# Signed adjacency copies picked by GpSimd in place of mask products on TensorE, in a four-layer graph network

## The chip, the cores and the metric

The kernel runs on one core of one Trainium2 chip. The metric is the device time of one execution in microseconds. A core has five engines that run side by side and meet at semaphores: TensorE (PE, matmuls into PSUM), VectorE (DVE), ScalarE (ACT), GpSimd (POOL) and SyncE (SP), which here issues all transfers.

## What is computed

32 graphs of 512 nodes with 256 features pass through four residual layers, each `x = x + layer(relu(layernorm(x)), adj)`, all in float32.

```python
# layer 0: (adj @ h + eps*h) @ W1 + b1 -> RMS norm -> silu -> @ W2 + b2       (W1: 256 -> 1024)
# layer 1: att = sigmoid(s1_i + s2_j) * adj * mask; rows normalised; att @ (h @ W.T + b)
# layer 2: 8 heads of 32 features:
scores = einsum('bhid,bhjd->bhij', q, k) / sqrt(HD) + edge_bias       # edge_bias = adj * W_e[head]
scores = where(adj_mask[:, None], scores, -inf)                       # adj_mask: adj != 0
attn   = softmax(scores); out = (attn @ v) @ W_o.T
# layer 3: d_i^-1/2 adj_ij d_j^-1/2 @ (h @ weight) + bias,  d = row sums of adj
```

The change concerns the edge bias and the mask of layer 2: a score gets W_e[head] times the adjacency value, and where the adjacency is zero it has to vanish from the softmax.

## The kernel before

A batch element (one graph) goes through a front half (layers 0 and 1) and a back half (layers 2 and 3). A phase works on three batch elements at once: the back half of t, the front half of tf = t + 1, and the load, norm and aggregation of nx = t + 2. There are 33 phases, those in the middle in a hardware loop. There is no scheduler: in each engine's block a function `phases(t, tf, nx)` calls the steps in an order written out by hand, and each engine runs its own list strictly in that order, with semaphore waits in between. So a step that waits holds up everything behind it on its engine.

The middle of a phase is a grid of 36 steps g = -4 to 31. At step g PE computes score tile g + 4 (head (g+4)//4, 128 rows, 512 columns) into one of two score banks, DVE's `bias` adds the adjacency, multiplies by the head's weight and takes the row extreme, ACT's `exps` makes the exponential, and PE turns tile g of the probabilities (`turn_probs`, four 128x128 transposes; a head's turns need all its four exps). ACT copies three of four turned tiles to `pT`, DVE the fourth. After head 3 and after head 7 the tiles are multiplied with the values (`attend`). Between these, the feed-forward part of layer 0 for tf runs in four tiles n, whose step u = g + 4 - 8n says what is due: hidden products at 0 and 1, squares on ACT, the norm factor on POOL (`hidden_norm`), `hidden` on DVE at 3, tanh and silu at 4 and 5, transposes of the hidden tile at 5 and 6, high and low halves at 6 and 7, down products in four quarters from 11, `update0` at 15. The last tile has its four quarters all at u = 8.

A score tile is two products, one for q k and one for the mask, which adds a huge value where the adjacency is zero. Its sign is the sign of the head's weight, because DVE's `bias` later multiplies the sum by that weight (`neg_w`) and takes a minimum:

```python
pe.matmul(SB_[i % 2][:, :], qk_stack[:, h % 4, 0, tile(n)], qk_stack[:, h % 4, 1, :], start=True, stop=False)
pe.matmul(SB_[i % 2][:, :], neg_mask[:, h, :], unlinked[:, n, :],
          start=False, stop=True).then_inc(sc_ps, 1)
```

`neg_mask` is a diagonal matrix per head, `unlinked` a bfloat16 map of the zero entries, made once per batch by `graph(t)` on DVE together with the row sums `deg`. The q and k of a head are stacked in four row groups by four SyncE transfers per head (`stack`), into one of four slots.

After the grid comes a stretch without scores: turn of the inverse sums, `attend(1)`, `project_o`, layer 1 of tf (`attend1`, `linear`), layer 3 of t (`aggregate3`, `project3`), the aggregation of nx in two halves (`aggregate(nx, 0)`, `aggregate(nx, 1)`), and the turn of hf for the next back half. Then the next phase begins with `project_qk`, `hidden(tf, 0, ...)` and `project_v`.

## Time and profile before

| | |
|---|---|
| median of 3 runs | 3797.84 us (3796.89 to 3798.93) |
| the profiled execution | 3793.83 us, its span 3792.0 us |
| PE busy | 3595.9 us, 95% |
| DVE busy | 2623.7 us, 69% |
| ACT busy | 2279.2 us, 60% |
| POOL busy | 772.2 us, 20% |
| mean granted clock of TensorE | 0.996 |

The span goes from the first to the last instruction of the core; 1.8 us of the execution's time lie around it. Busy shares overlap, since the engines work side by side. A matmul's duration in the trace runs from its issue to its modelled end, so for pipelined matmuls the distance from start to start says what one costs.

### The profile page before, as it was taken

The page shows a single profiled execution, that of the slowest core. Times are in us where ns is not written, and L with a number is a line of the kernel's source. Part 1 is how long each engine was busy: PE and PEld are TensorE (multiplying, and loading weights), DVE is VectorE, ACT ScalarE, POOL GpSimd, SP SyncE. Part 2 cuts the span into 40 slices and gives each one's busy share as a digit, 9 for nine tenths or more (in the row PEclk, how much of TensorE's full clock was granted, in tenths as well). Part 3 has the DMA queues.
Part 4 walks back from the last instruction along what each step waited for, and adds up shares of the span by engine and source line. Part 5 has one row for each costly group of instructions (what it writes and reads, how often), then busy time and mean ns, then how long its engine had stood idle before and what let it go on. Part 6 is the DMA issues. An engine that isn't in the chain of part 4 may idle for free.

```text
span 3792.0 us, 67268 instructions
## 1 busy us (share of the span) xinstructions
PE 3595.9 (95%) x19375; PEld 2445.7 (64%) x19596; DVE 2623.7 (69%) x6436; ACT 2279.2 (60%) x5029; POOL 772.2 (20%) x1611
## 2 busy tenths in 40 slices
PE   4899999999999999999999999999999999999997
PEld 3566666666666666666666666666666666666664
DVE  4676776666767766767767766667677667677664
ACT  2565666555666656666656665556666566666564
POOL 1122211222212222212222112222122222122210
PEclk9999999999999999999999999999999999999999
DMA  2232132322232322223321323222323222233212
GB/s 85 62 85 72 56 89 56 89 74 69 67 78 67 89 67 67 78 57 87 85 71 56 89 56 89 75 70 67 78 67 89 67 67 78 57 87 85 65 45 67
DMA packets 166936, 275.09 MB, mean 73 GB/s; under 512 B 23906, under 2 KB 59874, under 8 KB 166756
## 3 DMA queue, kind: packets, MB, share of 16 engines
q1 hardware_dynamic: 166756, 273.45, 26.7%
q14 instruction: 160, 1.31, 0.1%
q8 instruction: 20, 0.33, 0.0%
HBM read 122.37 MB, written 16.78 MB: 37 GB/s over the span
## 4 chain that ended last, share of the span: by engine, by line
PE 61%; issue 13%; DVE 12%; POOL 8%; ACT 5%; POOLq 0%; DMA 0%; DVEq 0%; SPq 0%; another core or an unknown queue 0%; ACTq 0%
PE turn L1213 9%; PE front L1026 7%; PE score L1203 6%; PE front L1027 6%; PE front L1028 6%; PE score L1204 4%; PE value L1228 3%; POOL small L374 3%; PE front L1056 3%; PE front L1079 3%; PE score L1177 3%; PE value L1189 3%; DVE pT L813 2%; ACT hf L500 2%; PE front L1068 2%
## 5 line engine op out<-in xcount | busy, mean ns | idle before, releaser
L588 ACT ACTIVATE prob<-prob,small 128x512 f32<-128x512 f32 x1024 | 736.1, 719 | 375.4 <-DVE small L888 373.8
L888 DVE CUSTOM_DVE_ANT_0 prob<-score,adj_sb,drv 128x512 f32<-128x512 f32 x1024 | 759.4, 747 | 224.8 <-PE score L1204 126.9
L1213 PE MATMUL turn<-ident,prob 128*128 128x128 f32 x4096 | 617.1, 276 | 14.6 <-ACT pT L597 8.7
L1213 PEld LDWEIGHTS turn<-ident,prob 128*128 128x128 f32 x4096 | 484.9, 141 | 134.8 <-issue 62.0
L597 ACT ACTIVATE pT<-turn 128x512 f32<-128x512 f32 x768 | 446.5, 584 | 144.6 <-PE turn L1213 144.6
L1203 PE MATMUL score<-qk_stack 128*128 128x512 f32 x1024 | 496.0, 488 | 31.5 <-DVE small L888 29.9
L1026 PE MATMUL front<-w_hi,s_hi 128*128 128x256 f32 x1024 | 353.0, 345 | 28.6 <-DVE x_in L792 28.6
L1204 PE MATMUL score<-unlinked,neg_mask 128*128 128x512 bf16 x803 | 313.6, 391 | 0.0
L680 DVE TENSOR_TENSOR s_lo<-front,s_hi 128x512 fp32r<-128x512 f32 x320 | 217.7, 680 | 102.7 <-ACT s_hi L486 102.6
L1027 PE MATMUL front<-w_lo,s_hi 128*128 128x256 f32 x1024 | 288.0, 281 | 0.0
L1028 PE MATMUL front<-w_hi,s_lo 128*128 128x256 f32 x1024 | 287.6, 281 | 0.0
L1026 PEld LDWEIGHTS front<-w_hi,s_hi 128*128 128x128 f32 x1024 | 196.0, 191 | 114.2 <-issue 52.6
L1228 PE MATMUL value<-pT,vals 128*32 128x512 f32 x2048 | 252.9, 600 | 5.1 <-issue 5.1
L421 POOL TENSOR_TENSOR inv_x<-small,drv 128x128 f32<-128x128 f32 x256 | 94.7, 401 | 784.0 <-DVE small L904 784.0
L1056 PE MATMUL front<-adjT_f,hid 128*128 128x512 f32 x512 | 232.0, 596 | 20.2 <-ACT hid L500 18.0
L486 ACT ACTIVATE s_hi<-front 128x512 fp32r<-128x512 f32 x320 | 187.5, 586 | 98.4 <-PE front L1111 94.5
L398 POOL TENSOR_TENSOR small<-small 128x1 f32<-128x1 f32 x128 | 24.7, 193 | 1083.3 <-ACT aside L529 1083.3
L773 DVE SCALAR_TENSOR_TENSOR hid<-front,small,rmsw_b 128x512 f32<-128x512 f32 x256 | 180.1, 745 | 88.8 <-POOL small L402 88.8
L1254 PE MATMUL score<-prob,hb 128*128 128x512 f32 x512 | 234.3, 601 | 4.5 <-ACT hb L500 4.5
L1203 PEld LDWEIGHTS score<-qk_stack 128*128 128x128 f32 x1024 | 195.0, 190 | 60.2 <-DVE small L888 54.5
L1111 PE MATMUL front<-pT,hf 128*128 128x512 f32 x512 | 227.5, 597 | 1.6 <-DVE pT L813 1.6
L897 DVE COPY pT<-turn 128x512 f32<-128x512 f32 x256 | 175.9, 687 | 75.8 <-PE turn L1213 73.9
(160 smaller groups left out, 7447.2 us busy)
## 6 DMA issues: line engine op xcount, KB each, us to landing
qk_stack<-qk SPq DMA_DIRECT2D x1024, 128.0 KB, 2.4
adjT_f<-in_adjT SPq DMA_DIRECT2D x32, 1024.0 KB, 5.0
adj_sb<-in_adj SPq DMA_DIRECT2D x32, 1024.0 KB, 7.9
prob<-in_adjT SPq DMA_DIRECT2D x32, 1024.0 KB, 5.4
x_new<-in_x SPq DMA_DIRECT2D x32, 512.0 KB, 3.7
out<-x_out SPq DMA_DIRECT2D x32, 512.0 KB, 3.1
pT<-in_W SPq DMA_DIRECT2D x2, 1024.0 KB
rmsw_b<-in_rmsw SPq DMA_DIRECT2D x1, 512.0 KB
```

What stands on the lines that cost most here:

```text
L588: act.activation(prob[:, i % 8, :], prob[:, i % 8, :], ACT.Exp, bias=nmax[:, h, n:n + 1], scale=-1.0, accum_out=prsum[:, h, n:n + 1]).then ...
L597: act.activation(pT[:, h % HG, j, :], TB[k % 2][:, :], ACT.Copy).then_inc(pT_act, 1)
L888: dve.tensor_tensor_reduce(out=prob[:, i % 8, :], in0=SB_[i % 2][:, :], in1=adj_sb[:, n, :], scale=neg_w[:, h:h + 1], scalar=3e38, op0=ALU ...
L1026: pe.matmul(ps, a[0], b[0], start=start, stop=False)
L1027: pe.matmul(ps, a[0], b[1], start=False, stop=False)
L1028: return pe.matmul(ps, a[1], b[0], start=False, stop=stop)
L1056: last = pe.matmul(FB[d][:, :], h0[:, m, tile(d)], adjT_f[:, m, :], start=(m == 0), stop=(m == NT - 1))
L1203: pe.matmul(SB_[i % 2][:, :], qk_stack[:, h % 4, 0, tile(n)], qk_stack[:, h % 4, 1, :], start=True, stop=False)
L1204: pe.matmul(SB_[i % 2][:, :], neg_mask[:, h, :], unlinked[:, n, :], start=False, stop=True).then_inc(sc_ps, 1)
L1213: last = pe.transpose(TB[k % 2][:, tile(n)], prob[:, (4 * h + n) % 8, tile(j)], ident[:, :])
L1228: last = pe.matmul(VB[HD * h:HD * h + HD, :], vals[:, j, P * g + HD * h:P * g + HD * h + HD], pT[:, h, j, :], start=(j == 0), stop=(j == N ...
L1254: last = pe.matmul(SB_[d][:, :], hb[:, m, tile(d)], adjT_b[:, m, :], start=(m == 0), stop=(m == NT - 1))
```

## The change

`unlinked`, `neg_mask` and the mask product go. Instead DVE makes two maps per batch, both with the adjacency where there is an edge, and where there is none +1e37 in one and -1e37 in the other. They stand side by side in `edges`; the loaded adjacency itself is turned into one of them. For each of the 32 score tiles GpSimd copies the tile of the map that fits the sign of the head's weight (`below`, read once into registers) into one of three buffers `edge`, and `bias` adds that. The row sums and the maps are made at the end of the phase before, when the element is still tf.

Further: `tile_steps` begins two steps earlier (u = g + 6 - 8n) with the transposes of the hidden tile at 6 and 7 and its halves at 7 and 8, and the last tile's quarters are spread over two steps; `aggregate(nx, 1)` moves from the end of a phase to behind `project_qk(tf, 0, ...)` of the next; `project_v(t, 1)` moves to step -2; `project_qk` writes into the turn banks; q and k of the second group of heads come a step later; there are three stack slots instead of four; `x_new` lies in a part of `pT`, so that the load of x waits for the last `attend`, behind the stack transfers and the two adjacency loads in SyncE's order; and `restore_diagonal` moves with the aggregation. Cut to the core:

```diff
         x2 = sb("x2", [P, NT, D])
-        adj_sb = sb("adj_sb", [P, NT, N])
-        unlinked = sb("unlinked", [P, NT, N], BF16)
+        edges = sb("edges", [P, 2, NT, N])
+        adj_sb, edges_neg = edges[:, 0, :, :], edges[:, 1, :, :]
+        edge = sb("edge", [P, 3, N])
         hb = sb("hb", [P, NT, D])
         bT = sb("bT", [P, DT, N])
         qk = sb("qk", [P, 4, N], F32R)
         x_out = sb("x_out", [P, NT, D], over="qk")
-        qk_stack = sb("qk_stack", [P, 4, 2, N], F32R)
+        qk_stack = sb("qk_stack", [P, 3, 2, N], F32R)
         vals = sb("vals", [P, NT, D])
         a3_hi = sb("a3_hi", [P, DT, N], F32R, over="vals")
...
-            return [(n, g + 4 - 8 * n) for n in range(NT) if 0 <= g + 4 - 8 * n < 16]
+            return [(n, g + 6 - 8 * n) for n in range(NT) if 0 <= g + 6 - 8 * n < 17]
         def quarters(n, u):
             if n == NT - 1:
-                return range(4) if u == 8 else ()
+                return (2 * u - 18, 2 * u - 17) if u in (9, 10) else ()
             return (u - 11,) if 11 <= u < 15 else ()
         GRID = range(-4, 4 * H)
-        Q1_STEP, K1_STEP = 0, 3
+        Q1_STEP, K1_STEP = 1, 4
+        def stack_slot(h):
+            return h % 3, 64 * (3, 3, 2)[h % 3], 64 * (h // 3 + 1)
         def linear_bank(n):
...
-            def back2(t):
...
@@ -314,6 +310,15 @@
                     if tf is not None:
                         load_adj(tf)
                 if nx is not None:
+                    sp.wait_ge(b2_added, at(tf, 1, 1))
+                    unregistered(sp)
+                    sp.wait_ge(f_norm["ready"], at(tf, 8, 4))
+                    unregistered(sp)
+                    if t is not None:
+                        sp.wait_ge(av_ps, at(t, 8, 8))
+                        unregistered(sp)
+                    load_x(nx)
                     sp.wait_ge(att_ready, at(tf, 4, 4))
                     unregistered(sp)
...
                 pool.wait_ge(deg_ready, at(t, 1, 1))
+                if later(t):
+                    pool.wait_ge(out_ready, at(t, 4, 0))
                 pool.tensor_tensor(dege, deg, wide(k_deg, NT), ALU.add).then_inc(deg_eps, 1)
                 pool.wait_ge(deg_eps, at(t, 1, 1))
                 pool.tensor_tensor(dinv, dege, wide(k_mhalf, NT), ALU.pow).then_inc(dinv_ready, 1)
+            def pick_edges(t, i):
+                h, n = divmod(i, NT)
+                if h == 0:
+                    pool.wait_ge(edges_ready, at(t, 4, n + 1))
+                if i >= 3:
+                    pool.wait_ge(biased, at(t, 32, i - 2))
+                elif later(t):
+                    pool.wait_ge(out_ready, at(t, 4, 0))
+                unregistered(pool)
+                pool.tensor_copy(edge[:, i % 3, :], edges[:, bass.ds(sign_of[h], 1), n, :].rearrange("p o n -> p (o n)")).then_inc(edge_picked, 1)
             def widen_inverse(t, g):
...
             def phases(t, tf, nx):
-                if t is not None:
+                b, f = t is not None, tf is not None
+                if b:
+                    for i in range(3):
+                        pick_edges(t, i)
                     degrees(t)
-                if tf is not None:
+                if f:
                     hidden_norm(tf, 0)
-                    hidden_norm(tf, 1)
-                if t is not None:
-                    widen_inverse(t, 0)
-                if tf is not None:
-                    hidden_norm(tf, 2)
-                    hidden_norm(tf, 3)
+                for i in range(3, 4 * H):
+                    if b:
+                        pick_edges(t, i)
+                    if f and i % 8 == 2 and i >= 8:
+                        hidden_norm(tf, i // 8)
+                    if b and i == 21:
+                        widen_inverse(t, 0)
                 if t is not None:
                     widen_inverse(t, 1)
...
                     act.wait_ge(av_ps, at(t, 8, j + 1))
+                if h == HG - 1 and j == 0:
+                    act.wait_ge(b2_added, B if isinstance(t, int) and t > B - 3 else at(t, 1, 2))
...
                 if f:
+                    aggregated(tf, 1)
+                if b:
+                    values(t, 0)
+                if f:
                     square(tf, 0, 0)
-                if b:
-                    values(t, 0)
-                if f:
                     square(tf, 0, 1)
-                if b:
-                    values(t, 1)
                 for g in GRID:
                     if f:
                         for n, u in tile_steps(g):
@@ -620,10 +647,12 @@
                                 square(tf, n, u - 1)
                             elif u in (4, 5):
                                 tanh(tf, n, u - 4)
-                            elif u in (6, 7):
-                                hidden_hi(tf, n, u - 6)
+                            elif u in (7, 8):
+                                hidden_hi(tf, n, u - 7)
                     if b and g + 4 < 4 * H:
                         exps(t, g + 4)
+                    if b and g == -2:
+                        values(t, 1)
                     if b and g >= 0 and g % 4 != DVE_TURN:
                         turned_probs(t, g // 4, g % 4)
...
-            def graph(t):
-                dve.wait_ge(adj_loaded, at(t, 16, 16))
-                if later(t):
-                    dve.wait_ge(sc_ps, at(t, 32, 0))
-                    dve.wait_ge(dinv_ready, at(t, 1, 0))
-                dve.tensor_scalar(unlinked[:, :, :], adj_sb[:, :, :], 0.0, None, ALU.is_equal).then_inc(unlinked_ready, 1)
-                dve.tensor_reduce(deg, adj_sb[:, :, :], AX.X, ALU.add).then_inc(deg_ready, 1)
+            def degree(tf):
+                dve.wait_ge(adj_loaded, at(tf, 16, 16))
+                if later(tf):
+                    dve.wait_ge(dinv_ready, at(tf, 1, 0))
+                dve.tensor_reduce(deg, adj_sb, AX.X, ALU.add).then_inc(deg_ready, 1)
+            def far_nodes(tf):
+                dve.tensor_scalar(edges_neg, adj_sb, 0.0, BIG, ALU.is_equal, ALU.mult).then_inc(far, 1)
+            def edges_below(tf):
+                dve.wait_ge(far, at(tf, 1, 1))
+                for n in range(NT):
+                    dve.tensor_tensor(edges_neg[:, n, :], adj_sb[:, n, :], edges_neg[:, n, :], ALU.add).then_inc(edges_neg_ready, 1)
+            def edges_above(tf):
+                dve.wait_ge(deg_ready, at(tf, 1, 1))
+                for n in range(NT):
+                    dve.wait_ge(edges_neg_ready, at(tf, 4, n + 1))
+                    dve.scalar_tensor_tensor(out=adj_sb[:, n, :], in0=adj_sb[:, n, :], scalar=2.0, in1=edges_neg[:, n, :],
+                                             op0=ALU.mult, op1=ALU.subtract).then_inc(edges_ready, 1)
             def turned(t):
...
             def turned_probs(t, h):
                 if h == HG:
                     dve.wait_ge(av_ps, at(t, 8, DVE_TURN + 1))
+                if h == HG - 1:
+                    dve.wait_ge(b2_added, B if isinstance(t, int) and t > B - 3 else at(t, 1, 2))
                 k = turn_of_prob[h, DVE_TURN]
...
                     attended1(tf, 0)
+                    degree(tf)
                     attended1(tf, 1)
                     factors1(tf)
                 if nx is not None:
                     diagonal(nx)
                 if f:
+                    far_nodes(tf)
                     update1(tf)
                     means(tf, 0, b_norm, norm_tiles(50))
                 if b:
                     gathered(t, 0)
                     gathered(t, 1)
+                if f:
+                    edges_below(tf)
                 if nx is not None:
                     aggregated(nx, 0)
                 if f:
                     turned(tf)
                 if b:
                     update3(t)
-                if nx is not None:
-                    aggregated(nx, 1)
-                    restore_diagonal(nx)
+                if f:
+                    edges_above(tf)
             stats0(0)
             diagonal(0)
             aggregated(0, 0)
-            aggregated(0, 1)
-            restore_diagonal(0)
             phases(None, 0, 1)
             phases(0, 1, 2)
             with dve.Fori(1, B - 2) as t:
...
                 if n == 0:
-                    pe.wait_ge(stacked[h % 4], at(t, 128, 64 * (h // 4 + 1)))
+                    s, per, k = stack_slot(h)
+                    pe.wait_ge(stacked[s], at(t, per, k))
                 if i == 0:
-                    pe.wait_ge(unlinked_ready, at(t, 1, 1))
                     pe.wait_ge(qk_lo_ready, at(t, 4, 2))
                 if i >= 2:
                     pe.wait_ge(biased, at(t, 32, i - 1))
-                pe.matmul(SB_[i % 2][:, :], qk_stack[:, h % 4, 0, tile(n)], qk_stack[:, h % 4, 1, :], start=True, stop=False)
-                pe.matmul(SB_[i % 2][:, :], neg_mask[:, h, :], unlinked[:, n, :],
-                          start=False, stop=True).then_inc(sc_ps, 1)
+                s = stack_slot(h)[0]
+                pe.matmul(SB_[i % 2][:, :], qk_stack[:, s, 0, tile(n)], qk_stack[:, s, 1, :], start=True, stop=True).then_inc(sc_ps, 1)
             def turn_probs(t, h, j):
...
                     project_qk(t, 0, 1)
                 if f:
+                    aggregate(tf, 1)
+                if b:
+                    project_v(t, 0)
+                if f:
                     hidden(tf, 0, 0)
-                if b:
-                    project_v(t, 0)
-                if f:
                     hidden(tf, 0, 1)
-                if b:
-                    project_v(t, 1)
                 for g in GRID:
                     if b and 0 <= g < 4 * H - 4:
                         scores(t, g + 4)
@@ -1294,16 +1337,20 @@
                         for n, u in tile_steps(g):
                             if n and u in (0, 1):
                                 hidden(tf, n, u)
-                            elif u in (5, 6):
-                                turn_hidden(tf, n, u - 5)
                             for q in quarters(n, u):
                                 down(tf, n, q)
                     if b and g < 0:
                         scores(t, g + 4)
+                    if b and g == -2:
+                        project_v(t, 1)
                     if b and g == Q1_STEP:
                         project_qk(t, 1, 0)
                     if b and g == K1_STEP:
                         project_qk(t, 1, 1)
+                    if f:
+                        for n, u in tile_steps(g):
+                            if u in (6, 7):
+                                turn_hidden(tf, n, u - 6)
                     if b and g >= 0:
                         turn_probs(t, g // 4, g % 4)
...
                     project3(t)
-                if nx is not None:
-                    aggregate(nx, 1)
```

## Rows read from the trace of the kernel before

**Rows 1.** Two stretches of one period: busy us, granted clock, DMA share, GB/s:

```profile
1061.48:1128.74 67.26, 64.49 (x402) 47.71 (x407) 49.85 (x115) 49.56 (x119) 7.00 (x22) 1.00 0.24 53
1013.64:1061.48 47.84, 47.08 (x206) 28.36 (x207) 31.60 (x85) 21.40 (x39) 17.10 (x30) 1.00 0.32 102
```

**Rows 2.** Waits of PE in one period: total us, times, longest:

```profile
PE front L1026 <- DVE x_in L792: 0.9, 1, 0.9
PE score L1203 <- DVE small L888: 0.9, 2, 0.6
```

**Rows 3.** Line L1204 by source: ns min/median/max, first and last start:

```profile
L1204 PEld LDWEIGHTS score<-unlinked,neg_mask x1024: 95/95/146, 141.0 to 3755.7; 128*128 128x128 bf16 x171
```

**Rows 4.** Timeline of PE in mid-stretch: start us, us, engine, line:

```profile
1078.88 0.48 PE L1203 MATMUL score<-qk_stack 128*128 128x512 f32 x1
1079.20 0.39 PE L1204 MATMUL score<-unlinked,neg_mask 128*128 128x512 bf16 x1
1079.43 0.60 PE L1213 MATMUL turn<-ident,prob 128*128 128x128 f32 x4
```

**Rows 5.** Groups by line and form, GpSimd: busy us, mean ns | idle before:

```profile
L431 POOL TENSOR_TENSOR pT<-pT 128x512 f32<-128x512 f32 x96 | 133.4, 1390 | 239.2 <-DVE pT L813 236.5
...
L354 POOL MEMSET ident<- 128x128 f32 x1 | 0.2, 204 | 0.3 <-POOLq L1377 0.3
```

**Rows 6.** Timeline of DVE at the attention products:

```profile
1020.20 1.42 DVE L813 SCALAR_TENSOR_TENSOR pT<-pT,mask_sb,adjT_f 128x512 f32<-128x512 f32 x2 [0.69 <-ACT pT L561]
1021.76 2.41 DVE L813 SCALAR_TENSOR_TENSOR pT<-pT,mask_sb,adjT_f 128x512 f32<-128x512 f32 x2 [0.15 <-ACT pT L561]
```

**Rows 7.** Timeline of GpSimd, two places:

```profile
1023.68 2.97 POOL L431 TENSOR_TENSOR pT<-pT 128x512 f32<-128x512 f32 x2 [0.71 <-DVE pT L813]
...
1042.89 2.78 POOL L389 TENSOR_TENSOR x_in<-x_new,b_b 128x256 f32<-128x256 f32 x4
```

**Rows 8.** Groups by line and form, DVE:

```profile
L888 DVE CUSTOM_DVE_ANT_0 prob<-score,adj_sb,drv 128x512 f32<-128x512 f32 x1024 | 759.4, 747 | 224.8 <-PE score L1204 126.9 <-remote 88.2
L680 DVE TENSOR_TENSOR s_lo<-front,s_hi 128x512 fp32r<-128x512 f32 x320 | 217.7, 680 | 102.7 <-ACT s_hi L486 102.6
...
L779 DVE SCALAR_TENSOR_TENSOR hid<-aside,hid 128x512 f32<-128x512 f32 x256 | 176.7, 690 | 63.0 <-ACT aside L536 62.6
...
L865 DVE TENSOR_REDUCE small<-adj_sb 128x4 f32<-128x2048 f32 x32 | 72.9, 2278 | 0.0
...
L864 DVE TENSOR_SCALAR unlinked<-adj_sb 128x2048 bf16<-128x2048 f32 x32 | 38.9, 1217 | 0.0
```

**Rows 9.** Groups by line and form, ScalarE:

```profile
L588 ACT ACTIVATE prob<-prob,small 128x512 f32<-128x512 f32 x1024 | 736.1, 719 | 375.4 <-DVE small L888 373.8
```

**Rows 10.** Timeline of PE in the second stretch:

```profile
1014.22 3.64 PE L1228 MATMUL value<-pT,vals 128*32 128x512 f32 x32
...
1048.10 3.60 PE L1056 MATMUL front<-adjT_f,hid 128*128 128x512 f32 x8
1051.53 3.60 PE L1177 MATMUL score<-bT,ws 128*128 128x512 f32 x8
...
1059.94 1.89 PE L1189 MATMUL value<-ws,bT 128*128 128x256 f32 x8
```

**Rows 11.** Timeline of DVE in the second stretch:

```profile
1027.24 1.38 DVE L727 BATCH_NORM_STATS2 small<-x_new 128x6 f32<-128x256 f32 x4
...
1032.11 0.69 DVE L680 TENSOR_TENSOR s_lo<-front,s_hi 128x512 fp32r<-128x512 f32 x1 [2.50 <-ACT s_hi L486]
...
1035.67 0.48 DVE L847 SCALAR_TENSOR_TENSOR pT<-bL_b,small,front 128x256 f32<-128x256 f32 x1 [0.29 <-PE front L1028]
...
1040.91 1.25 DVE L680 TENSOR_TENSOR a_lo<-score,a_hi 128x512 fp32r<-128x512 f32 x2
...
1046.15 0.68 DVE L869 COPY bT<-turn 128x512 f32<-128x512 f32 x1
```

**Rows 12.** Timeline of SyncE: the first stack transfers of a batch:

```profile
1056.81 5.20 SPq L291 DMA_DIRECT2D qk_stack<-qk  x8
```

74 lines of the change are left out of this document (33 added, 41 removed).

## Prediction

> **What bounds the kernel now.** The page comes first: it puts TensorE (PE) far ahead of the other engines in busy time, evenly over all slices, with most of the ending chain on it. So the next views are those that show whether PE ever waits. In the timeline the first aggregate product recurs every 115.1 us. I cut one such period at the first score product (1061.48) and at the transposes of the inverse (1128.74; a period earlier 1013.64). In [rows 1] the reader should see that in the score stretch of 67.3 us PE is idle for 2.8 us while DVE and ScalarE (ACT) have some 17 us free each, that in the other 47.8 us PE is idle for 0.8 us and DVE has 16 us free, and that the granted clock is full (1.00) in both. PE sets the pace of both stretches. The waits name the two main places where PE does stand: 0.9 us for the score ring (a score product needs the bias of two scores before to be done) and 0.9 us for the x_in update ahead of the last tile's down products [rows 2]. A saving on PE is real until DVE or the new GpSimd work takes over.
>
> **Removed: the mask product.** Each of the 1024 scores is two products; the second, L1204, goes. Its 1024 weight loads are all in the trace (some matmul records are missing), and they reach from 141.0 to 3755.7 us: 31 periods of 115.1 and 47 us of the last batch alone [rows 3]. A matmul's duration there is a latency; its cost is start to start. Score to mask takes 0.32 us, mask to the next transpose 0.23 us [rows 4]. The 0.32 is the score's own and stays; if the mask shares in it, the most that one can cost is its whole 0.39 us. I take 0.23: 32 x 0.23 = 7.4 us per batch (bound above 12.5, none below 7.4 while PE is the bound, and nothing at all where it is not).
>
> **Added on GpSimd: 32 picks per batch**, copies of 128x512 f32 out of one of two maps. No row shows a one-input copy. From below: a memset of 128 elements takes 0.20 us, so one of 512 between 0.2 and 0.8 us. From above: the two-input add of the same size, 1.39 us with its waits [rows 5]. A copy reads one operand, so it lies nearer to memset; I take 0.8 us and 0.1 us for the register that selects the map. That is 29 us in a stretch where GpSimd is busy for 7.0 us [rows 1]; with 1.39 us it would be 44.5 + 7, still under 60. Three buffers let a pick start when the bias three steps before is done, so each has about two steps (a step is 67.3 us over 36, 1.9 us) to spare. Queued behind a pick on GpSimd are the hidden-norm steps and the widening of the inverse. The norm of tile n stands behind pick 8n+2, released by bias 8n-1, while the squares it needs come a step later; the pick is over by then. Cost on the path: 0. The Trainium skill, page "GPSIMD Engine Reference", section 3.1 (elementwise accounting), gives 769 ns for a tight loop over 512 elements; as an estimate from that page 32 picks are 24.6 us, and its section 4.1 advises against elementwise work here for two inputs only. No run here shows it yet.
>
> **Port.** Where DVE's attention product (two SBUF inputs) runs alone, two take 1.42 us; beside GpSimd's add, two take 2.41 us [rows 6, 7]. So a two-input DVE operation beside GpSimd costs up to 0.5 us more. In the score stretch only the 8 silu products (L779) have two SBUF inputs; bias, hidden and the low halves read one operand from PSUM. 8 x 0.5 = 4 us at most on DVE, which then is at 49.9 + 4 = 54 of about 62 us: no bound. The Trainium skill, page "SBUF — State Buffer", section "SBUF: two separate sides", says that such an operation and a GpSimd one that reads SBUF exclude each other for the whole instruction. By that, a silu could wait a full pick, 8 x 0.9 = 7.2 us, 57 of 62.
>
> **Moved within the score stretch.** The front's steps come two places earlier, transposes of the hidden tile have two steps after silu instead of one, and the last tile's down products are spread over steps 27 and 28 with the previous x_in update at 25. The 0.9 us wait for x_in [rows 2] goes. But the feed-forward work of tile 0 now meets scores 0 to 3. Written out from the first score, with the durations of [rows 8, 9], each overlapping the next by some 0.07: bias 0 from 0.7 and bias 1 until 2.1 us, the two hidden products (three operands each, 1.4 together) until 3.4, bias 2 until 4.1, silu until 4.7, bias 3 until 5.4, exp until 6.1, and only then the first probability transpose at 6.3. PE has until then five scores (0.32 each), values 1 (1.54, moved in [rows 10]) and one group of hidden transposes (0.5, like that of [rows 4]): 3.7 us of work, so some 2.5 us idle against 0.9 us now. Plus 1.6 us (0 if the exp comes sooner, 3 if GpSimd is late with pick 3, which is queued behind hidden norm 0).
>
> **Moved and added in the other stretch (DVE).** Gone: the unlinked map, 1.22 us. The degree reduction, 2.28 us, goes between the two halves of attended1, where DVE waits 2.5 us for ScalarE [rows 8, 11]: 0. Without that cover it would delay the linear products by 2.3. far_nodes is a one-input tensor_scalar over 128x2048, like the unlinked map: 1.22 us ahead of update1, where DVE has 0.29 us idle. So the message product, on which the fourth linear product waits, and the means, the norm and the transposes of hf after it come 0.9 us later; PE is busy up to each of them now, so it loses 0.9 us. edges_below, 4 x 0.68 minus overlap = 2.5 us, starts when the low halves of the gather end (1042.2, then 1043.1) and meets GpSimd's b2 additions (2.78 us from 1042.89 [rows 7]); with 0.5 us each that is until 1047.5. Then T_lo and the copy of bT: 1048.7 instead of 1046.8 [rows 11]. Late next would be project_qk, since the second aggregation (3.43 us), which stood in between, now comes behind it: PE reaches it at 1048.1 + 0.9 = 1049.0 [rows 10]. Just hidden; I put down 0.4 us (2 if the additions and edges_below serialise fully). edges_above, four operations like L779 (2.5 us, 3.5 beside the first picks), delays qk_low, which is done at about 1055.6 against 1056.7. The first score then can start 4.7 us after the first stack issue, as now (1056.81 to 1061.48 [rows 12]), at 1060.4; PE comes at 1061.1, after second aggregation, values 0 and both hidden products. Hidden by those: 0; without them it would be 4.7 us. The aggregation itself, values 1 and the diagonal's return only change place.
>
> **Queues.** SyncE now has the x load behind the stack transfers and behind both adjacency loads (1 MB each), and lets it wait for the last attend, which ends at 1017.9 [rows 10]. In the second stretch the DMA engines moved 102 GB/s at a share of 0.32 [rows 1], so some 320 GB/s when busy: even if all 2.6 MB started then, x would be there at 1026, and its statistics start at 1027.2 [rows 11]. Hidden, with about 1 us left at worst. Three stack slots instead of four: head 3 waits for score 3 and its transfers land some 5 us later, at about 1070, when ScalarE wants to overwrite qk (step 2). Now four slots must land, 16 issues of 0.65 us from 1056.81 on [rows 12], so until about the same time: 0 to 1 us more, counted as 0.
>
> **Sum for a period.** 115.1 - 7.4 - 0.9 + 1.6 + 0.9 + 0.4 = 109.7 us, a gain of 5.4. Times 31: 167. The first and the last batch alone are not bound by PE; edges add some 3 us there. 3793.83 - 167 + 3 = 3630 for the profiled execution; the median of the runs lies 4 us above it, so 3634.
>
> **Rivals.**
> (A) The forecast: PE stays the bound with a few new waits. Period 108.3 to 111, time 3590 to 3674.
> (B) Nothing new stalls: 115.1 - 7.4 - 0.9, perhaps less a part of the 0.32: period near 106.7, 3540. For it: DVE's 16 us free in each stretch [rows 1]. Against: the written-out start of the stretch.
> (C) The port and the longer DVE queue eat half: silu waits a whole pick, edges_below and the b2 additions serialise, ramp 3 us. That is 2 to 3 us more than in A: period 112.5, 3720. For it: [rows 6, 7]; DVE at 57 of 62 us leaves no room for latencies, with a score ring of two. The rule of the Trainium skill named above (page "SBUF — State Buffer") speaks for this case.
> (D) Slower: GpSimd becomes the bound. With its 7 us of other work a pick above 1.7 us, address steps included, makes GpSimd the bound of a stretch of 62 us, above 1.9 us nothing of the gain is left, and at 2.2 us a stretch is 70.4 + 7 = 77 us, 10 us more per period: 4105. Against it: it is more than 1.39, the highest row for this size; for it: no row shows an access by register.
> (E) The products go but the chain score, bias, exp, transpose bounds each head: period about as before, 3798. Against: PE has at least 2.5 us of other work between the last score of a head and its first transpose.
>
> **How the numbers follow.** Chances: A 0.50, B 0.13, C 0.25, D 0.08, E 0.04. The forecast is A's 3634. Leaving out D and E and the outer part of B gives 3560 to 3740. 0.2% is 7.6 us, about what a measurement can tell from no change. Faster 0.88, same 0.03, slower 0.09.
>
> **What would show it.** Right: no L1204, a period near 110 us, PE still above 94%, picks of 0.6 to 1 us, no wait of bias for a pick in mid-stretch, PE idle 2 to 3 us between the first score and the first transpose, none before the last down products. Wrong: bias waiting on GpSimd at each step (D), silu near 1.2 us or DVE above 90% in the score stretch (C), project_qk waiting for bT, the first score waiting for its transfer, x statistics waiting for a DMA.

## The result: 1.4% slower, where 4.3% faster was forecast

The changed kernel takes 3850.68 us (median of 4 runs, 3846.67 to 3852.54) against 3797.36 us for the kernel before on the same chip (4 runs, 3795.54 to 3798.93). The ratio is 1.0139, 95% interval 1.0122 to 1.0157. It lies above the range given and on the other side of no change. One execution of e9 below took 11197.82 us at a granted clock of 0.446; it is the one that was profiled, so no wait of e9 is read here.

The page of the changed kernel, busy time by engine:

```profile
PE 3463.8 (90%) x18572; PEld 2357.4 (61%) x18572; DVE 2805.1 (73%) x6685; ACT 2289.3 (59%) x5029; POOL 1518.3 (39%) x2635
```

PE is busy for 132 us less than before in a span that is 59 us longer (3850.7 us). No engine is full: PE, the longest, is at 90%, and the rest of its time has to be looked for in waits between engines. The same cut of a period as in [rows 1], at the transposes of the inverse and at the first score product:

```profile
1033.46:1081.69 48.23, 46.72 (x203) 27.20 (x202) 37.69 (x93) 21.13 (x38) 21.75 (x33) 1.00 0.35 106
1081.69:1149.74 68.05, 60.17 (x382) 45.78 (x381) 49.52 (x115) 50.13 (x120) 25.75 (x49) 1.00 0.23 48
sum 116.28, PE 106.89 PEld 72.98 DVE 87.21 ACT 71.25 POOL 47.51; mean PE 53.44 PEld 36.49 DVE 43.60 ACT 35.63 POOL 23.75
```

The period is 116.3 us where 109.7 was forecast. The stretch without scores should have been 47.84 + 0.9 + 0.4 - 1.54 (values 1 has left it) = 47.6 us and is 48.2. The score stretch should have been 67.26 - 7.4 - 0.9 + 1.6 + 1.54 = 62.1 us and is 68.05: 6.0 of the 6.6 us that the period is off lie here, and here PE is idle for 7.9 us against 2.8 in [rows 1]. The waits of PE in one period (those of [rows 2] on the old lines), total us, times, longest:

```profile
PE turn L1259 <- ACT prob L613: 3.3, 3, 1.3
PE score L1251 <- DVE small L930: 1.5, 3, 0.8
PE front L1115 <- DVE s_lo L706: 1.4, 1, 1.4
PE front L1073 <- DVE s_lo L706: 0.6, 1, 0.6
...
PE turn L1259 <- DVE pT L941: 0.4, 1, 0.4
PE front L1073 <- DVE pT L872: 0.4, 1, 0.4
```

The wait for x_in is gone as forecast, and behind it stands one of 0.6 us for the low halves. New are three waits of the probability transposes for an exponential, at the steps 0, 8 and 24, and one of the next tile's hidden product for the low halves of the tile before. At step 16 there is none: PE has a part of `attend` ahead of the transposes there.

What GpSimd and the port were feared for did not come. Groups by line and form, GpSimd, busy us, mean ns, idle before and its releasers:

```profile
L429 POOL COPY edge<-edges 128x512 f32 x1024 | 695.4, 688 | 1048.2 <-DVE small L930 935.1 <-DVE edges L905 104.4 <-issue 7.5
L395 POOL TENSOR_TENSOR x_in<-x_new,b_b 128x256 f32<-128x256 f32 x128 | 116.6, 941 | 0.0
```

The same view for DVE:

```profile
L930 DVE CUSTOM_DVE_ANT_0 prob<-score,edge,drv 128x512 f32<-128x512 f32 x1024 | 756.6, 742 | 491.3 <-PE score L1251 484.3 <-issue 4.9 <-POOL edge L429 1.8
L804 DVE SCALAR_TENSOR_TENSOR hid<-aside,hid 128x512 f32<-128x512 f32 x256 | 182.8, 714 | 76.5 <-ACT aside L560 76.4
L905 DVE SCALAR_TENSOR_TENSOR edges<-edges 128x512 f32<-128x512 f32 x128 | 106.0, 888 | 0.0
L898 DVE TENSOR_TENSOR edges<-edges 128x512 f32<-128x512 f32 x128 | 95.5, 806 | 0.0
L892 DVE TENSOR_SCALAR edges<-edges 128x2048 f32<-128x2048 f32 x32 | 39.0, 1220 | 0.0
```

A pick takes 0.69 us, and of all idle time ahead of 1024 biases 1.8 us is put down to a pick; of the 1048 us that GpSimd itself idles ahead of picks 935 are waits for biases and 104 for the maps. So GpSimd is early nearly every time.

One place that shows how the score stretch loses time is step 5 of eight (g = 5, 13, 21), where DVE has a tile's two hidden products. DVE at g = 5, start us and us:

```profile
1099.40 0.75 DVE L930 CUSTOM_DVE_ANT_0 prob<-score,edge,drv 128x512 f32<-128x512 f32 x1 [1.55 <-PE score L1251]
...
1100.08 1.40 DVE L798 SCALAR_TENSOR_TENSOR hid<-front,small,rmsw_b 128x512 f32<-128x512 f32 x2
1101.40 0.68 DVE L941 COPY pT<-turn 128x512 f32<-128x512 f32 x1
1102.00 0.68 DVE L706 TENSOR_TENSOR qk<-value,qk 128x512 fp32r<-128x512 f32 x1
1102.60 0.74 DVE L930 CUSTOM_DVE_ANT_0 prob<-score,edge,drv 128x512 f32<-128x512 f32 x1
...
1103.26 0.69 DVE L804 SCALAR_TENSOR_TENSOR hid<-aside,hid 128x512 f32<-128x512 f32 x1
1103.87 0.75 DVE L930 CUSTOM_DVE_ANT_0 prob<-score,edge,drv 128x512 f32<-128x512 f32 x1
```

and PE, from the last score of head 2 to the first transpose of that head:

```profile
1101.46 0.48 PE L1251 MATMUL score<-qk_stack 128*128 128x512 f32 x1
...
1103.40 0.50 PE L1251 MATMUL score<-qk_stack 128*128 128x512 f32 x1 [0.33 <-DVE small L930]
...
1106.03 0.65 PE L1259 MATMUL turn<-ident,prob 128*128 128x128 f32 x4 [1.00 <-ACT prob L613]
```

DVE first waits 1.55 us for a score, since PE is at k's projection for the second group of heads (four products, 1.9 us); then in one step it gets two hidden products, the copy of a turned tile and a low half of k (this one only at g = 5, once in a period), so that two biases stand 3.2 us apart, with silu behind. The head's last score is issued at 1101.46, its bias starts only at 1103.87, its exponential follows behind a tanh on ACT, and PE, which needs all four exponentials of a head for the first transpose, idles 1.0 us at 1106.03. DVE has 18 us free in this stretch, but not at this place.

### The profile page after: what moved, and what is told of

It reads as the page before. It is cut to its first block, busy times and chain, and to the rows that moved or that the text cites. A ratio compares the mean times of both kernels' runs of the same rounds, so it can differ in the third digit from the quotient of the medians.

```text
span 3850.7 us, 68842 instructions
## 1 busy us (share of the span) xinstructions
PE 3463.8 (90%) x18572; PEld 2357.4 (61%) x18572; DVE 2805.1 (73%) x6685; ACT 2289.3 (59%) x5029; POOL 1518.3 (39%) x2635
## 4 chain that ended last, share of the span: by engine, by line
PE 44%; issue 18%; DVE 18%; POOL 9%; ACT 8%; DVEq 1%; POOLq 1%; DMA 0%; SPq 0%; ACTq 0%
PE turn L1259 7%; PE score L1251 4%; PE front L1073 4%; PE front L1075 4%; PE front L1074 4%; PE value L1274 3%; POOL small L380 3%; PE value L1223 3%; PE front L1103 3%; ACT prob L613 3%; PE turn L1223 3%; PE value L1236 3%; DVE pT L838 2%; DVE prob L930 2%; ACT hf L524 2%
## 5 line engine op out<-in xcount | busy, mean ns | idle before, releaser
L930 DVE CUSTOM_DVE_ANT_0 prob<-score,edge,drv 128x512 f32<-128x512 f32 x1024 | 756.6, 742 | 491.3 <-PE score L1251 484.3
L429 POOL COPY edge<-edges 128x512 f32 x1024 | 695.4, 688 | 1048.2 <-DVE small L930 935.1
L1259 PE MATMUL turn<-ident,prob 128*128 128x128 f32 x4096 | 628.2, 278 | 139.6 <-ACT prob L613 108.9
L1259 PEld LDWEIGHTS turn<-ident,prob 128*128 128x128 f32 x4096 | 467.8, 141 | 264.6 <-issue 93.1
L1251 PE MATMUL score<-qk_stack 128*128 128x512 f32 x1024 | 489.3, 483 | 55.5 <-DVE small L930 48.3
L1073 PE MATMUL front<-w_hi,s_hi 128*128 128x256 f32 x1024 | 295.6, 289 | 20.0 <-DVE s_lo L706 18.4
L1251 PEld LDWEIGHTS score<-qk_stack 128*128 128x128 f32 x1024 | 195.0, 191 | 109.7 <-DVE small L930 93.1
L804 DVE SCALAR_TENSOR_TENSOR hid<-aside,hid 128x512 f32<-128x512 f32 x256 | 182.8, 714 | 76.5 <-ACT aside L560 76.4
L451 POOL TENSOR_TENSOR pT<-pT 128x512 f32<-128x512 f32 x96 | 133.5, 1391 | 239.1 <-DVE pT L838 236.4
L1073 PE MATMUL front<-w_hi,T_hi 128*128 128x512 f32 x512 | 204.3, 399 | 0.5 <-DVE T_lo L706 0.5
```

The costliest lines, as they stand in the source:

```text
L429: pool.tensor_copy(edge[:, i % 3, :], edges[:, bass.ds(sign_of[h], 1), n, :].rearrange("p o n -> p (o n)")).then_inc(edge_picked, 1)
L930: dve.tensor_tensor_reduce(out=prob[:, i % 8, :], in0=SB_[i % 2][:, :], in1=edge[:, i % 3, :], scale=neg_w[:, h:h + 1], scalar=3e38, op0=A ...
L1073: pe.matmul(ps, a[0], b[0], start=start, stop=False)
L1251: pe.matmul(SB_[i % 2][:, :], qk_stack[:, s, 0, tile(n)], qk_stack[:, s, 1, :], start=True, stop=True).then_inc(sc_ps, 1)
L1259: last = pe.transpose(TB[k % 2][:, tile(n)], prob[:, (4 * h + n) % 8, tile(j)], ident[:, :])
```

## The experiments

All times are medians of the named kernel. e1, e4, e13, e14, e17 and e18 leave out a part of the computation, so they are no kernels to use; they only price that part. "New order" is the changed kernel's place of the front's steps in the grid, "old order" that of before. The period's length is read from the recurrence of the first score product.

**e1. The mask product alone, out of the kernel before.**

```diff
-pe.matmul(SB_[i % 2][:, :], qk_stack[:, h % 4, 0, tile(n)], qk_stack[:, h % 4, 1, :], start=True, stop=False)
-pe.matmul(SB_[i % 2][:, :], neg_mask[:, h, :], unlinked[:, n, :], start=False, stop=True).then_inc(sc_ps, 1)
+pe.matmul(SB_[i % 2][:, :], qk_stack[:, h % 4, 0, tile(n)], qk_stack[:, h % 4, 1, :], start=True, stop=True).then_inc(sc_ps, 1)
```

> The kernel before with nothing changed but that the mask product of each score is left out (its maps are still made, so softmax is not masked). If the order of the grid is what cost the change its gain (theory 1), the old order has room: PE falls by 7.4 us per period and the time to 3570 to 3620. If a head's chain of score, bias and exp bounds the stretch whatever the order (theory 2), little comes: 3740 to 3800.

3720.24 us, ratio 0.9801 (0.9785 to 0.9817): 75 us, a third of the 229 us that 31 x 7.4 would be, and between the two expectations. The period goes from 115.1 to 112.4, 2.7 us less. Its waits of PE over the whole run (the second figure is the number of them):

```profile
PE front L1079 <- DVE hid L779: 57.0, 121, 4.1
PE turn L1211 <- ACT prob L588: 43.8, 67, 1.8
PE score L1203 <- DVE small L888: 42.7, 96, 1.2
```

The same three groups in the kernel before:

```profile
PE score L1203 <- DVE small L888: 29.9, 65, 1.2
...
PE front L1079 <- DVE hid L779: 23.5, 36, 4.1
...
PE turn L1213 <- ACT prob L588: 5.2, 5, 2.0
```

Freed of the mask product, PE comes earlier to the hidden transposes, the exponentials and the score ring, and waits there: 85 us of the missing 154 are in these three groups. Another 9 us are clock: in eight of its periods the clock falls to half of full for a while, and they are 1.2 us longer than the others of 112.4 us; in the kernel before no period has it. Where the other 60 us are is not shown; the record of a score is 0.48 us long where one costs 0.32, so the start of a wait counts as busy and the waits printed are rather too small.

**e2. The new order alone, in the kernel before, mask product kept; e3. The old order in the changed kernel.** The edit of e3, on all engines alike (e2 is its reverse; the places of GpSimd's hidden norm and of the last tile's x_in update follow and are not printed):

```diff
-            return [(n, g + 6 - 8 * n) for n in range(NT) if 0 <= g + 6 - 8 * n < 17]
+            return [(n, g + 4 - 8 * n) for n in range(NT) if 0 <= g + 4 - 8 * n < 16]
-                return (2 * u - 18, 2 * u - 17) if u in (9, 10) else ()
+                return range(4) if u == 8 else ()
-        Q1_STEP, K1_STEP = 1, 4
+        Q1_STEP, K1_STEP = 0, 3
...
-            if u in (7, 8): hidden_lo(tf, n, u - 7)          # ACT's hidden_hi likewise
+            elif u in (6, 7): hidden_lo(tf, n, u - 6)
-            if u in (6, 7): turn_hidden(tf, n, u - 6)        # behind the score
+            elif u in (5, 6): turn_hidden(tf, n, u - 5)      # ahead of the score
```

> The kernel before, mask products kept, with only the new order of the grid: feed-forward steps two places earlier, hidden transposes behind, last quarters spread, q and k of the second group one step later. Theory 1 (in the new order DVE's hidden products and its pT copy fall into the same step, bias comes late, the first transpose of a head waits): 2 to 6 us more per period, 3860 to 3980. Theory 2 and theory 3 (GpSimd's picks and the longer DVE list of the map): 3780 to 3800, less the 0.9 us wait for x_in.

> The changed kernel with picks and all else kept, but the feed-forward steps, the hidden transposes, the last quarters and the q and k steps where they were before (hidden norm behind pick 8n+4 to match). Theory 1: 3620 to 3700. Theories 2 and 3: 3830 to 3870.

e2 takes 3947.69 us, ratio 1.0406 (1.0388 to 1.0423), 153 us slower with the order alone. e3 takes 3730.24 us, ratio 0.9829 (0.9813 to 0.9845): the changed kernel with the old order is 120 us faster than the changed kernel, and 1.7% faster than the one before. Both kernels agree: the order is the loss. e2 lies in theory 1's range; e3 lies 30 us above its upper end and 100 us below that of the other theories. PE's longest waits in e2, beside those of the kernel before that are printed at e1:

```profile
PE turn L1213 <- ACT prob L588: 76.7, 98, 2.0
PE score L1203 <- DVE small L888: 58.6, 65, 1.6
PE front L1068 <- ACT s_hi L486: 33.9, 30, 1.1
```

PE's waits in e3:

```profile
PE front L1126 <- DVE hid L804: 67.5, 129, 4.1
PE turn L1259 <- ACT prob L613: 45.1, 67, 2.0
PE front L1073 <- ACT s_hi L510: 29.1, 31, 1.0
PE score L1251 <- DVE small L930: 26.8, 33, 1.2
```

and in the changed kernel, the same view:

```profile
PE turn L1259 <- ACT prob L613: 108.9, 99, 1.6
PE score L1251 <- DVE small L930: 48.3, 95, 1.6
PE front L1115 <- DVE s_lo L706: 45.2, 33, 1.4
...
PE front L1073 <- DVE s_lo L706: 18.4, 29, 0.6
...
PE front L1126 <- DVE hid L804: 11.4, 8, 4.1
```

The new order does what its extra step is for: the wait of the hidden transposes for silu goes from 67.5 to 11.4 us. It pays with 64 us at the exponentials, 21 at the ring and 45 at the low halves, which now come at u = 7 and 8, one step ahead of the next tile's hidden products instead of two.

**e4. No picks.** `bias` adds one fixed map.

```diff
-                        pick_edges(t, i)
...
-                dve.tensor_tensor_reduce(out=prob[:, i % 8, :], in0=SB_[i % 2][:, :], in1=edge[:, i % 3, :],
+                dve.tensor_tensor_reduce(out=prob[:, i % 8, :], in0=SB_[i % 2][:, :], in1=edges_neg[:, n, :],
```

> The changed kernel without the 32 picks of GpSimd: bias reads one of the two maps directly, so heads with the other sign get the wrong mask. All else is kept. Theory 3 (picks late, port contention): 3700 to 3780. Theories 1 and 2: 3835 to 3851, since bias hardly ever waits for a pick in the trace and silu is only 0.02 us longer.

3856.73 us, ratio 1.0162 (1.0146 to 1.0179): within 0.2% of the changed kernel, 6 us above the expectation of theories 1 and 2 and far from that of theory 3. The 1024 copies on GpSimd cost nothing on the path.

**e5 to e7, e9, e10, e15, e16. One move at a time inside the new order.**

```diff
e5:  -DVE_TURN = 1                       +DVE_TURN = 0      # DVE's copy in steps 0 and 4, not 1 and 5
e6:  -(n, g + 6 - 8 * n)                 +(n, g + 4 - 8 * n)   # the shift by two alone undone; GpSimd's hidden norm follows, in e15 and e16 too
e7:  -Q1_STEP, K1_STEP = 1, 4            +Q1_STEP, K1_STEP = 0, 3
e9:  -turn_hidden at 6, 7; halves 7, 8   +turn_hidden at 5, 6; halves 6, 7
e10: -tanh ahead of the step's exp       +tanh behind it
e15: -(n, g + 6 - 8 * n)                 +(n, g + 7 - 8 * n)
e16: -(n, g + 6 - 8 * n)                 +(n, g + 5 - 8 * n)
```

> The changed kernel, with DVE's share of the turned probabilities moved from the second turn of a head to the first: the copy leaves the steps 1 and 5 of eight, where it meets the hidden products, the x_in update and the low halves, for steps 0 and 4, where DVE has only bias. If the collision on DVE is what the new order costs (theory 1a): 3760 to 3815. If it is the shift as such, that is which PE work stands beside which wait (theory 1b): 3835 to 3860.

> The changed kernel with only the shift of the feed-forward steps undone (u = g + 4 - 8n again, hidden norm behind pick 8n+4); hidden transposes at 6 and 7, halves at 7 and 8, spread quarters and q, k steps stay new. If the shift carries the cost: 3720 to 3760. If it is the transposes a step later or the q and k steps: 3800 to 3850.

> The changed kernel with q and k of the second group projected at steps 0 and 3 again, so that the low half of k leaves DVE's step 5, where it stands behind hidden products and pT copy. Happens once per period, of four such steps. Theory 1a: 3820 to 3845. If q and k steps are nothing: 3851.

> The changed kernel with only the hidden transposes (u 5 and 6 again) and their halves (6 and 7 again) one step earlier. In the changed kernel the next tile's hidden product waits 1.4 us per period for the low half that frees its bank, and a down product 0.6 us for another. If these waits are the cost of the later halves (theory 1d): 3780 to 3815. If they only stand in for the head's chain: 3840 to 3851, with the wait of the first transpose for exp grown by as much.

> The changed kernel with ScalarE's exp ahead of tanh within a step. In the new order both tanh of a tile stand in the steps 6 and 7 of eight, ahead of the exp on which the next head's first transpose waits (3.3 us per period, three waits). If that place is the cost (theory 1c): 3770 to 3815. If exp is late because bias is late: 3840 to 3860, and silu waits longer for tanh.

> The changed kernel with the feed-forward steps one step earlier still (u = g + 7 - 8n, hidden norm behind pick 8n+1). The burst then stands in steps 4 to 6 of eight, a step away from the next head's first transposes. Theory 1e: 3760 to 3825. If each step earlier costs by itself: 3880 to 3920.

> The changed kernel with the feed-forward steps one step later (u = g + 5 - 8n, hidden norm behind pick 8n+3). The burst stands in steps 6, 7 and 8: the hidden products and the first tanh are still ahead of the last exp. Theory 1e: 3830 to 3930, no gain. If each step later is a gain by itself: 3790.

| | us | ratio to before, 95% | against the changed kernel |
|---|---|---|---|
| e5 | 3905.59 | 1.0284 (1.0266 to 1.0301) | +55 |
| e6 | 4049.76 | 1.0664 (1.0646 to 1.0682) | +199 |
| e7 | 3926.09 | 1.0339 (1.0321 to 1.0356) | +75 |
| e9 | 3886.55 | 1.0233 (1.0216 to 1.0250) | +36 |
| e10 | 4151.34 | 1.0932 (1.0914 to 1.0951) | +301 |
| e15 | 3912.04 | 1.0305 (1.0288 to 1.0323) | +61 |
| e16 | 3942.98 | 1.0381 (1.0363 to 1.0398) | +92 |

Every one is slower, so undoing one move gives nothing back by itself, and each theory that one collision makes the loss fell. Only e15 lies in one of its ranges (3880 to 3920); the other six lie above all of theirs. In e5 the step read above is rid of its copy, and the waits for exponentials stay at 107.8 us, while transposes wait 23 us each for two other copies. In e7 the exponentials' wait falls from 108.9 to 60.2 and from 99 times to 59: with q's product for the second group back at step 0, ahead of the first transposes, the wait there is gone; but that product now waits 25.8 us for the copies of values, the ring's wait rises from 48.3 to 72.2 and the halves' from 45.2 to 69.2. In e6 the two stand at 174.3 and 175.4 us. In these three, undoing one move shifts the waits to other places; all of them together (e3) take most of them away.

A part of two of these times is clock. The mean granted clock is 0.954 in e6 and 0.956 in e10 against 0.987 in the changed kernel, and in each of their 31 periods it falls to half of full for a while. PE does the same products and is busy for 3524.5 and 3614.9 us against 3463.8, 61 and 151 us more. So the +199 and the +301 are not the price of the waits alone; how much of each is clock is not separated.

**e8, e11, e12. The rest of the old order.** e8 is e3 with the second aggregation back at the end of the phase; e12 is e8 with values 1, the first squares and the first hidden product at their old places too; e11 is e3 with the hidden transposes behind the score, as in the change.

> The kernel of e3 (picks, old order of the grid) with the second aggregation of the next element back at the end of the phase. In e3 ScalarE stands 6.1 us per period for the stored output before it may write qk; the aggregation covers that. If the moved aggregation costs (theory 4): 3690 to 3715. If the wait is hidden behind PE's own work, as the trace of the changed kernel suggests: 3725 to 3740.

> The kernel of e3 (picks, old order), with the hidden transposes still in their old steps but behind the down products of the step instead of ahead of them. In e3 they wait 1.8 us per period for silu. 3680 to 3715 if the downs fill that wait; 3725 to 3735 if the wait moves to the exps.

> The kernel of e8 (old order, second aggregation at the end of the phase) with the second half of the values back ahead of the grid as well, so that the whole order is the old one and only mask product, picks, maps and slots differ from the kernel before. e8 waits 1.3 us per period for the first stacked q and k. If values 1 covers that: 3740 to 3790. If edges_above, which stands ahead of the low halves of q and k, is what is late: 3800 to 3830.

e8: 3827.02 us, ratio 1.0078 (1.0061 to 1.0095), 97 us behind e3 and above both expectations. In it the first score waits for the stack transfers, 44.9 us in total, and 23 of its 31 periods contain a fall of the clock to half and are 116.3 us long where seven at full clock are 114.7: some 37 us more. e12: 3767.49 us, 0.9919 (0.9903 to 0.9936), as expected if values 1 covers that wait. e11: 3728.65 us, 0.9819 (0.9803 to 0.9836), the same as e3, as expected if the wait only moves. So the aggregation between q, k and the first score is the cover that the prediction named, and moving it together with values 1 is worth 37 us (e12 to e3). e3 and e11 are the fastest of the versions that compute everything.

**e13, e14. tanh and silu on one column of 512, in the new and in the old order.**

```diff
-                act.activation(aside[:, :], hid[:, N * c:N * c + N], ACT.Tanh).then_inc(tanh_done, 1)
+                act.activation(aside[:, 0:1], hid[:, N * c:N * c + 1], ACT.Tanh).then_inc(tanh_done, 1)
```

> The changed kernel with tanh and silu done for one column of each half tile only (the rest of the activation is left out); all steps and waits stay. Theory 1e, the burst of hidden, tanh and silu right ahead of a head's first transposes is what the new order costs: 3690 to 3760, most of the 120 us between the two orders comes back. If the new order costs through PE's own sequence or through the banks: 3800 to 3840.

> The kernel of e3 (picks, old order) with the same small tanh and silu. Theory 1e: 3680 to 3715, 20 to 50 us less than e3, since only the hidden transposes wait for silu there (1.8 us per period). If the burst costs the same in both orders: as much less than e3 as e13 is less than the changed kernel.

3794.79 us (0.9992, 0.9982 to 1.0002), 5 us below the second expectation, and 3671.86 us (0.9669, 0.9652 to 0.9685). Both orders gain alike, 56 and 58 us, and their distance stays: 123 us. That tanh and silu in front of a head's last bias make the difference between the orders fell too.

**e17, e18. All feed-forward steps of DVE and ACT on one column, in both orders** (in the 29 phases of the hardware loop).

```diff
-                    dve.scalar_tensor_tensor(out=hid[:, cs], in0=FB[c][:, :], scalar=rms[:, n:n + 1], ...
+                    dve.scalar_tensor_tensor(out=hid[:, cs], in0=FB[c][:, 0:W], scalar=rms[:, n:n + 1], ...
                    # W = 1 in the hardware loop, N = 512 outside; cs is W wide too; the other kinds alike
```

> The changed kernel, but in the batches of the hardware loop the feed-forward steps on VectorE and ScalarE (squares, hidden products, tanh, silu, high and low halves) work on one column instead of 512, so most of their values are left out; all products on TensorE, all waits and the order stay. In the changed kernel they take some 2.8 us of 8 steps on VectorE beyond the biases twice over (1.4 hidden, 1.4 silu, 1.4 halves) and about 4.3 us on ScalarE. Theory S (the order costs time because this work now meets the last biases and exponentials of every second head): with it nearly gone, new and old order differ by less than 30 us (under 1 us per period), and the transposes' wait for exponentials (108.9 us) falls below 30. Rival P (it is TensorE's own order against the chain of score, bias and exponential, whatever the feed-forward work on the other engines): the two orders still differ by 80 to 125 us. Time of this run: by S 3640 to 3680, by P 3700 to 3760.

> The same shrinking of the feed-forward steps on VectorE and ScalarE, in the changed kernel with the old order of the grid (3730.2 us with the full work, 3671.9 us with small tanh and silu). By S 3610 to 3660 and within 30 us of the other run. By P also 3610 to 3660, but 80 to 125 us below the other run.

3697.73 us (0.9735, 0.9719 to 0.9752) and 3663.57 us (0.9646, 0.9630 to 0.9662). The distance falls from 120 to 34 us. PE's waits in e17:

```profile
PE turn L1269 <- ACT prob L620: 77.2, 99, 1.6
PE score L1261 <- DVE small L940: 28.9, 37, 1.6
PE front L1125 <- ACT s_hi L514: 25.4, 29, 0.9
```

and in e18:

```profile
PE turn L1269 <- ACT prob L620: 44.2, 67, 1.7
PE front L1083 <- DVE x_in L827: 27.1, 29, 0.9
PE score L1261 <- DVE small L940: 26.9, 33, 1.2
PE value L1233 <- DVE qk L925: 25.9, 31, 1.7
```

From e13 to e17 squares, hidden products and halves go as well: 97 us in the new order, and only 8 in the old one (e14 to e18). So the time that these three kinds of steps take on DVE and ACT makes 89 us of the distance: in the old order it is nearly hidden, in the new one it is on the path. (The pair before was shrunk in all 32 batches, this one in 29, so these are good to a few us.) Where it shows on PE is not where S had it. From e13 to e17 the wait for exponentials hardly moves, 79.5 to 77.2 us, while the ring's falls from 48.2 to 28.9, those for the high halves from 43.6 to 25.4 (next tile's hidden product) and from 26.2 to 9.3 (down product), and that for DVE's copy of a turned tile from 13.4 to 0.7; together 69 of the 97 us.

Of the 34 us left, the largest part is the exponentials' wait, 77.2 against 44.2: three in a period instead of two, and the third is the first head's, the start of the grid that the prediction priced. Another 5 us come before the first score of the first batch (148.6 us against 143.6); against it e18 has a wait for the low half of q that e17 has only once, 25.9 us. The time of e17 lies between the two expectations, above the 3680 of S and below the 3700 of P; that of e18 is 4 us above both. The distance of 34 is near S's 30, but S's second sign, a wait for exponentials below 30 us, failed. So the size speaks for feed-forward work of DVE and ACT, the place for the ring and the banks of the halves, and the wait at the start of the grid stays whatever that work is.

## Why the prediction was wrong

Step by step, the time of a period, forecast beside measured (kernels before, e1, e3, after: 115.1, 112.4, 112.8, 116.3 us):

| part | forecast | measured | by |
|---|---|---|---|
| mask product goes | -7.4 | -2.7 | e1 |
| picks, maps, aggregation and values moved | +0.9 + 0.4 | +0.4 | e3 against e1 |
| front's steps in the new order | +1.6 - 0.9 | +3.5 | after against e3 |
| sum | -5.4 | +1.2 | |

The three errors, 4.7, -0.9 and 2.8 us, make the 6.6 us by which the period is off, and 31 x 6.6 = 205 us. The profiled execution is off by 222 us (3852.54 against 3630). Of the rest 8 us are clock (last section) and 8 are the edges: the first score comes 8 us later than before (148.4 against 140.6) and the last batch takes 3 us more from its first score on, where 3 were counted for both.

Two steps failed, and it took both to make the kernel slower: with the mask product as forecast the sum would be -7.4 + 0.4 + 3.5 = -3.5 us, with the front's steps as forecast -2.7 + 0.4 + 0.7 = -1.6 us. (The split goes along one path, mask product first; the order alone costs 4.4 us in the kernel before, by e2, against 3.5 here.)

**The step that missed a cost is "Moved within the score stretch".** The prediction wrote out the feed-forward work on DVE and ACT against PE only for tile 0, at the start, and took the other 28 steps as the old ones moved along. The written part was right: PE idles 0.81 + 0.33 + 1.29 = 2.43 us before the first transpose, forecast 2.5; the 1.29 is gone in e7, where q's product for the second group is back ahead of the first transposes. The -0.9 for x_in was half right, since 0.6 us for the low halves took its place. What it left at 0 was the move of tiles 1 to 3 against the heads. A shift by two steps of a pattern of eight changes which bias and which exponential stands behind hidden products and halves, and one step more for transposes and halves takes a step from the next tile's hidden product. The new order as a whole costs 120 us by e3 and 153 by e2; of the 120, 31 x 2.8 = 87 us were not priced. By e13, e14, e17 and e18 the work of squares, hidden products and halves on DVE and ACT makes 89 of the 120.

**The mask product was mis-sized, and this is the larger error.** "A saving on PE is real until DVE or the new GpSimd work takes over" was judged by DVE's free time per stretch (17 us). Free time in a stretch says nothing of a chain: score, bias, exponential and transposes run with a ring of two banks and a head's four exponentials as a gate, and of the 7.4 us taken from PE 4.7 did not reach the period (e1); 85 of these 154 us stand as waits at those gates. The start to start of 0.23 us is what the trace shows for the product; the bound "none below 7.4 while PE is the bound" had a condition that failed after a third of the saving. This is the mechanism of (E) working in part, at up to 4.7 of 7.4 us. What (E) was given as its counter-argument, at least 2.5 us of other work on PE between a head's last score and its first transpose, holds where it was read: in the rows of PE above it is 4.57 us less 1.33 of idle time, 3.2 us. The chain took longer, 4.6 us, because the bias came 2.4 us after its score was issued.

**What was right.** The picks cost 0 on the path (e4), at 0.69 us against 0.8 taken; (D) is refuted. The estimate from the Trainium skill, page "GPSIMD Engine Reference", section 3.1, 769 ns for 512 elements, lies 12% above the measured 688 ns. The x_in wait went. project_qk waits for bT only in the first batch (1.5 us), the first score for its transfer only in the last, which has no second aggregation ahead of it (5.9 us), and the statistics of x never wait for their load. The cover of the first score by the second aggregation is real (e8). The wait for the message product behind far_nodes is 0.4 us where 0.9 was put down.

**The port, (C).** Beside GpSimd the operations with two SBUF inputs do grow: the b2 additions from 0.73 to 0.94 us, edges_above 0.89 us where 0.69 was the row's, edges_below 0.81 against 0.68. e4 tells what the picks have to do with it: without them edges_above takes 0.68 us and edges_below still 0.81, beside the additions. But silu, the one kind in the score stretch, goes only from 690 to 714 ns (691 in e4), though in the trace it lies beside GpSimd work for 0.38 us on the mean; why it grows so little is open. In e3, the fastest order, it takes 767 ns. By the rule of the Trainium skill, page "SBUF — State Buffer", section "SBUF: two separate sides", a silu could have waited a full pick, 0.69 us; the mean of 256 shows 0.02 us, and the longest silu of the changed kernel is 0.83 us, of e3 1.04 us. So no silu here grew by a full pick. C's mechanism is not the loss, and its 3720 us was missed by 131.

**The cases.** None of the five held the measured time. The rival that ended on the slower side was GpSimd's, the part most visibly new; a case "the order written out by hand no longer fits" was missing, although [rows 9] shows ScalarE waiting 374 us for biases and [rows 8] DVE 127 us for scores, the links of just that chain.

**Open.** Which of squares, hidden products and halves carries most of the 89 us is not separated, and neither is why all seven single moves are slower; where the waits go was read for e5, e6 and e7 alone, and the share of the clock in e6 and e10 is not separated. 60 us of e1's missing saving stand in no printed wait.

## What to carry to other kernels

When a hand-written order of steps is shifted against another, write out one full pattern of it for each in-order engine, with the waits at every gate (here the head's fourth exponential and the next tile's low halves), not only its start. An engine at 95% gives back a saving only as far as the chains through its neighbours allow: take the work away alone, in the old order, and read the waits, before the gain is counted. And a change that brings new work and a new order is worth timing with the old order first: here that version is 1.7% faster than before where the whole is 1.4% slower.

## What the runs showed of the hardware

The granted clock fell behind a start of the scores in the changed kernel. Windows of PE in one such place, busy us, granted clock, DMA share, GB/s:

```profile
847.10:851.10 4.00, 3.19 (x15) 1.00 0.92 201
851.10:855.10 4.00, 2.27 (x13) 0.98 0.63 133
855.10:859.10 4.00, 4.00 (x12) 0.59 0.05 9
859.10:863.10 4.00, 4.00 (x22) 1.00 0.00 0
```

After the stretch in which PE was busy for only 2.27 of 4 us (the start of the scores with its 2.4 us of idle time), the mean clock of the next 4 us is 0.59, so it stands mostly at its lower level of 1.2 GHz, and then at full again. Five of the 31 periods show this and are 1.3 to 1.7 us longer, 8 us in all; in the kernel before, which idles 0.9 us there, no period does. All periods of the changed kernel have the same idle time, so it alone does not say in which the clock falls. In e1, e6, e8 and e10 the clock falls in more of the periods, 8, 31, 23 and 31, at a mean granted clock of 0.989, 0.954, 0.979 and 0.956. So idle time at one place can cost again behind it.

ScalarE waits 6.1 us in each period ahead of the first q for the stored output, which lies over `qk`. In the kernel before this wait stands once, 5.8 us. Here it is hidden, since the first score comes without a wait; the prediction had not seen it.
